# GNN and mixture-of-experts layer: VectorE takes all the scaling and adding ahead of the routing, with w2's loads and the counts moved

## The reference, cut to what matters

```python
x = x + gnn(layernorm(x), edges)            # x: 6250 x 256, 100000 edges, 8 heads of 32
x = x + ffn(layernorm(x)[None])[0]

def gnn(x, ...):                            # attention over the edges, summed by target node
    out = segment_sum(attn_exp * h[src], dst) / (segment_sum(attn_exp, dst) + 1e-10)
    return out + x
def ffn(x, ...):                            # 16 experts, hidden 512, top 2
    gate_logits = x @ gate_w + gate_b
    topk_vals, topk_idx = top_k(gate_logits, 2)
    moe = sum_k softmax(topk_vals)_k * (relu(x @ w1[e_k] + b1[e_k]) @ w2[e_k] + b2[e_k])
    return layernorm(x + moe) * gamma + beta
```

## Time and profile before

| | |
|---|---|
| median of 3 runs | 1956.9 us (1956.38 to 1959.61) |
| the profiled execution | 1957.13 us, of which its span 1955.3 us |
| sum over edges ends, routing stage begins | about 1326.5 us from the start of the span |
| first gather of rows by slot issued | 1456.3 us |
| `layer2` of the first slot tile begins | 1471.4 us |
| busy over the span | PE 78%, POOL 61%, DVE 60%, ACT 40% |

### The profile page before, as it was taken

The page is one execution under the profiler, slowest core; times in us unless marked ns, Lnnn a source line. Parts: engine busy times, 40 slices in busy tenths (PEclk is TensorE's granted clock), DMA queues, the critical chain, the costliest instruction groups (busy, mean ns, idle before and its releaser), DMA issues.

```text
span 1955.3 us, 28026 instructions
## 1 busy us (share of the span) xinstructions
PE 1515.8 (78%) x6735; PEld 1115.6 (57%) x6735; DVE 1177.6 (60%) x3451; ACT 774.8 (40%) x2346; POOL 1200.1 (61%) x1186
## 2 busy tenths in 40 slices
PE   7647777777777777777777777774959999999976
PEld 5524444444444444444444444443848999999963
DVE  7746666666666666666666666669873444333338
ACT  3434444444444444444444444342622333333326
POOL 1366666666666666666666666637354767656757
PEclk9856666666766666676666667675559999999987
DMA  8544444444444444444444444422957878888876
GB/s 240 151 113 119 114 113 116 115 120 116 113 115 115 121 117 112 115 117 118 120 111 116 116 118 118 112 60 89 281 162 191 220 212 212 211 205 206 220 170 199
DMA packets 167873, 283.93 MB, mean 145 GB/s; under 512 B 31671, under 2 KB 94504, under 8 KB 167592
## 3 DMA queue, kind: packets, MB, share of 16 engines
q0 software_dynamic: 62144, 143.99, 31.3%
q1 hardware_dynamic: 104532, 138.03, 23.0%
q10 hardware_dynamic: 1044, 0.13, 0.0%
HBM read 240.71 MB, written 42.16 MB: 145 GB/s over the span
## 4 chain that ended last, share of the span: by engine, by line
PE 64%; DVE 22%; issue 7%; DVEq 4%; another core or an unknown queue 2%; DMA 1%; ACT 0%; SPq 0%; ACTq 0%; POOL 0%; POOLq 0%
PE bank L1063 29%; PE bank L1204 10%; PE bank L1216 10%; DVE region L1533 5%; PE bank L1052 4%; PE bank L1088 2%; DVE region L1531 2%; DVE z L1486 2%; DVEq L496 2%; PE bank L993 2%; PE bank L1049 2%; PE bank L1113 2%; DVE z L1493 1%; DVE z L1498 1%
## 5 line engine op out<-in xcount | busy, mean ns | idle before, releaser
L898 POOL DMA_INDIRECT region<-node_rows,region x832 | 788.2, 947 | 449.1 <-issue 221.5
L1063 PE MATMUL bank<-region 128*128 128x264 f32 x1664 | 740.0, 593 | 70.9 <-DVE region L1533 68.0
L1063 PEld LDWEIGHTS bank<-region 128*128 128x128 f32 x1664 | 440.1, 290 | 211.6 <-issue 124.9
L1533 DVE TENSOR_TENSOR region<-region,bank 128x264 f32 x728 | 310.6, 427 | 343.3 <-PE bank L1063 261.1
L756 ACT ACTIVATE neg_max<-bank 128x1 f32<-128x1 f32 x104 | 17.8, 171 | 711.7 <-PE bank L1088 588.1
L1519 DVE TENSOR_TENSOR region<-region,bank 128x512 f32<-128x512 f32 x416 | 265.2, 678 | 7.9 <-issue 7.9
L746 ACT ACTIVATE region<-iota_row,region 128x128 f32<-128x128 f32 x832 | 262.7, 386 | 0.0
L830 ACT ACTIVATE region<-bank,b_col 128x128 f32<-128x128 f32 x452 | 128.7, 368 | 311.9 <-PE bank L1204 224.1
L974 POOL DMA_INDIRECT sum_rows<-region,row_u x113 | 179.6, 1590 | 111.8 <-DVE region L1953 52.8
L1204 PEld LDWEIGHTS bank<-region 128*128 128x128 f32 x1808 | 220.3, 192 | 6.3 <-issue 0.4
L1204 PE MATMUL bank<-region 128*128 128x128 f32 x1808 | 220.8, 275 | 0.2 <-issue 0.2
(11 more groups left out here) (247 smaller groups left out, 1619.4 us busy)
## 6 DMA issues: line engine op xcount, KB each, us to landing
region<-in_L_ffn_w SPq DMA_DIRECT2D x129, 512.0 KB, 8.3
region<-dloc_rows SPq DMA_DIRECT2D x104, 256.0 KB
region<-node_rows,region POOLq DMA_INDIRECT x832
node_rows<-region SPq DMA_DIRECT2D x12, 528.0 KB, 4.0
y_rows<-region SPq DMA_DIRECT2D x7, 896.0 KB, 6.0
sum_rows<-region SPq DMA_DIRECT2D x7, 896.0 KB, 7.5
region<-in_x SPq DMA_DIRECT2D x5, 896.0 KB, 11.0
region<-sum_rows SPq DMA_DIRECT2D x5, 896.0 KB, 11.2
```

What stands on the lines that cost most here:

```text
L898: p.indirect_dma_start(gathered[g % SLOTS][:, j, :], None, node_rows, bass.IndirectOffsetOnAxis(src_idx[:, k:k + 1], 0)).then_inc(row_in[g ...
L1063: pe.matmul(bank[AGG_BANKS[k % AGG]][:, 0:ROW], onehot[:, (g % 3) * GROUP + j, :], gathered[g % SLOTS][:, j, :], start=True, stop=True).th ...
L1533: v.tensor_tensor(rows, rows, new, ALU.add).then_inc(acc_add)
```

## The change

DVE scales and adds all eight groups, in their order, and POOL none of them. The second part of the inverted sums is now tiles 7 to 13, the third tiles 14 to 48. The normalised rows get a third buffer, in the place of the gathered rows of the first seven tiles, so ACT waits for the store of three batches before, not two. SP stores all seven batches of rows first; then it waits until all additions are made, loads experts 2 to 12 of w2, waits until the batches in the third buffer have left it, and loads experts 0 and 1. Experts 13 to 15 are loaded ahead of the stage as before. In DVE's program `best_two(0)` and `choose(0)` stand behind the variance of group 7 instead of group 6. In PE's program the count of set 0 stands in group 7 behind its fifth tile's transposes (before: in group 5), and that of set 1 behind the last tile of the gate (before: in group 7, fourth tile).

```diff
-C_DVE, C_POOL = (0, 1, 2, 4), (3, 5, 6, 7)
-C_PARTS = ((0, 7), (14, TILES), (7, 14))
+C_DVE = (0, 1, 2, 3, 4, 5, 6, 7)
+C_PARTS = ((0, 7), (7, 14), (14, TILES))
+Y_RING = 3
...
-        y_all = region2[:, 0:2 * BATCH * F_IN].rearrange("p (s t f) -> p s t f", s=2, f=F_IN)
+        Y_AT = (region2[:, 0:BATCH * F_IN], region2[:, BATCH * F_IN:2 * BATCH * F_IN], region1[:, 0:BATCH * F_IN])
+        y_all = [y.rearrange("p (t f) -> p t f", f=F_IN) for y in Y_AT]
...
-            w2_at = 0
             for q in range(BATCHES):
                 store_y0(q)
-                i = q + 1
-                if i in C_POOL:
-                    d.wait_ge(x1_pool, 2 * C_POOL.index(i) + 2)
-                else:
-                    d.wait_ge(x1_dve, 2 * C_DVE.index(i) + 2)
-                while w2_at < behind_sums and (q == BATCHES - 1 or (w2_at + 1) * FC * F_IN <= (q + 1) * BATCH * ROW):
-                    load_w2(w2_at)
-                    w2_at += 1
+            d.wait_ge(x1_dve, len(X1))
+            behind_y = -(-BATCH * F_IN // (FC * F_IN))
+            for expert in range(behind_y, behind_sums):
+                load_w2(expert)
+            for q in range(BATCHES):
+                if q % Y_RING == 2:
+                    d.wait_ge(y_out[2], y_landed(q))
+            for expert in range(behind_y):
+                load_w2(expert)
...
-                if q >= 2:
-                    s.wait_ge(y_out[q % 2], y_landed(q - 2))
+                if q >= Y_RING:
+                    s.wait_ge(y_out[q % Y_RING], y_landed(q - Y_RING))
...
-            for n in range(len(C_POOL)):
-                residual(n)
...
-                    if i == 5 and t == t0 + 3:
+                    if i == 7 and t == t0 + 4:
                         count_choices(0)
-                    if i == 7 and t == t0 + 3:
-                        count_choices(1)
                 gate_logits(t1 - 1)
+            count_choices(1)
...
-            sums_part(1)
+            gathered_sums(1)
             shift_c(0)
-            inverse_sums(1)
-            gathered_sums(1)
             add_x(1)
             stats_c(1)
-            sums_part(2)
-            inverse_sums(2)
+            sums_part(1)
+            inverse_sums(1)
             shift_c(1)
             gathered_sums(2)
             add_x(2)
             stats_c(2)
-            stats_c(3, 2)
+            sums_part(2)
+            shift_c(2)
+            inverse_sums(2)
+            gathered_sums(3)
+            add_x(3)
+            stats_c(3)
             gathered_sums(4)
             shift_c(3)
             add_x(4)
             stats_c(4)
+            gathered_sums(5)
+            shift_c(4)
+            add_x(5)
             stats_c(5)
-            shift_c(4)
+            gathered_sums(6)
+            shift_c(5)
+            add_x(6)
             stats_c(6)
+            gathered_sums(7)
+            shift_c(6)
+            add_x(7)
+            stats_c(7)
             best_two(0)
-            shift_c(5)
+            shift_c(7)
             choose(0)
-            stats_c(7)
-            shift_c(6)
             v.wait_ge(pool_consts, POOL_CONSTS["empty"])
             v.tensor_copy(empty, empty_i).then_inc(c_const_step)
             slots(0)
             for q in range(*SETS[0]):
                 tile_hots(q)
-            shift_c(7)
             pair_firsts(0)
```

More of the change, by code:

```diff
@@ L52 @@
 FC = HIDDEN // P
-assert sum(C_TILES) == TILES and sorted(C_DVE + C_POOL) == list(range(len(C_TILES)))
+assert sum(C_TILES) == TILES and sorted(C_DVE) == list(range(len(C_TILES)))
 assert TILES % BATCH == 0 and SLOT_TILES <= P and ROW <= 512
@@ L301, in build_program @@
         late_step, late_exp, late_mm = sem("late_step"), sem("late_exp"), sem("late_mm")
-        y_out = [sem(f"y_out{i}") for i in range(2)]
-        sums_step, x1_dve, x1_pool = sem("sums_step"), sem("x1_dve"), sem("x1_pool")
+        y_out = [sem(f"y_out{i}") for i in range(Y_RING)]
+        sums_step, x1_dve = sem("sums_step"), sem("x1_dve")
         y0_ok, y0_tr, y0t_ok = sem("y0_ok"), sem("y0_tr"), sem("y0t_ok")
@@ L339, in build_program @@
         SUMS = at([(name, n) for n in range(len(C_PARTS)) for name in ("sums", "rsum")])
+        X1 = at([("scaled", 0), ("added", 0), ("scaled", 1), ("added", 1), ("scaled", 2), ("added", 2),
+                 ("scaled", 3), ("added", 3), ("scaled", 4), ("added", 4), ("scaled", 5), ("added", 5),
+                 ("scaled", 6), ("added", 6), ("scaled", 7), ("added", 7)])
         WEIGHT = at([("gap", 0), ("gap", 1)] + [(n, s) for s in range(2) for n in ("gap1", "weight0", "weight1")])
@@ L402, in y_landed @@
         def y_landed(q):
-            return 32 * (q // 2 + 1) + (16 if q % 2 == 0 else 0)
+            return 32 * (q // Y_RING + 1) + (16 if q % Y_RING == 0 else 0)
         A_NORMS = len(A_TILES)
@@ L451, in p_bank @@
             return bank[Z_BANKS[g % 2]][:, GROUP * AD:GROUP * (AD + HEADS)].rearrange("p (j h) -> p j h", h=HEADS)
-        y_all = region2[:, 0:2 * BATCH * F_IN].rearrange("p (s t f) -> p s t f", s=2, f=F_IN)
+        Y_AT = (region2[:, 0:BATCH * F_IN], region2[:, BATCH * F_IN:2 * BATCH * F_IN], region1[:, 0:BATCH * F_IN])
+        assert BATCH * F_IN <= C_PARTS[0][1] * ROW
+        y_all = [y.rearrange("p (t f) -> p t f", f=F_IN) for y in Y_AT]
         yt_buf = region2[:, 2 * BATCH * F_IN:2 * BATCH * F_IN + 2 * F_IN].rearrange("p (s f) -> p s f", f=F_IN)
@@ L597, in store_y0 @@
                 d.wait_ge(y0_ok, (q + 1) * BATCH)
-                d.dma_start(rows_of(y0_rows, q)[:, :, 0:F_IN], y_all[:, q % 2, :, :]).then_inc(y_out[q % 2], 16)
-                d.dma_start(rows_of(sum_rows, q), y_all[:, q % 2, :, :]).then_inc(y_out[q % 2], 16)
+                y = y_all[q % Y_RING]
+                d.dma_start(rows_of(y0_rows, q)[:, :, 0:F_IN], y[:, :, :]).then_inc(y_out[q % Y_RING], 16)
+                d.dma_start(rows_of(sum_rows, q), y[:, :, :]).then_inc(y_out[q % Y_RING], 16)
             def store_weights(s):
@@ L644, in sync_program @@
             d.wait_ge(slot_step, SLOT["expert_row"])
-            for q in (BATCHES - 2, BATCHES - 1):
-                d.wait_ge(y_out[q % 2], y_landed(q))
+            for q in range(BATCHES - Y_RING, BATCHES):
+                d.wait_ge(y_out[q % Y_RING], y_landed(q))
             experts = None
@@ L781, in norm @@
                 q = t0 // BATCH
-                if q >= 2:
-                    s.wait_ge(y_out[q % 2], y_landed(q - 2))
+                if q >= Y_RING:
+                    s.wait_ge(y_out[q % Y_RING], y_landed(q - Y_RING))
                 for t in range(t0, t0 + n):
-                    s.activation(y_all[:, q % 2, t % BATCH, :], x_all[:, t, :], ACT.Identity,
+                    s.activation(y_all[q % Y_RING][:, t % BATCH, :], x_all[:, t, :], ACT.Identity,
                                  bias=shift[:, t:t + 1], scale=rstd[:, t:t + 1]).then_inc(y0_ok)
@@ L899, in gpsimd_program @@
                                          bass.IndirectOffsetOnAxis(src_idx[:, k:k + 1], 0)).then_inc(row_in[g % SLOTS], 16)
[L902 to L913, removed]
             def choice_one_hots(q):
@@ L949, in gpsimd_program @@
             p.wait_ge(slot_step, SLOT["token"])
-            for q in (BATCHES - 2, BATCHES - 1):
-                p.wait_ge(y_out[q % 2], y_landed(q))
+            for q in range(BATCHES - Y_RING, BATCHES):
+                p.wait_ge(y_out[q % Y_RING], y_landed(q))
             p.wait_ge(weight_out, 32)
@@ L1124, in norm_transposes @@
                     ins = pe.transpose(bank[4 + t % 2][:, c * P:(c + 1) * P],
-                                       y_all[:, t // BATCH % 2, t % BATCH, c * P:(c + 1) * P], ident[:, :])
+                                       y_all[t // BATCH % Y_RING][:, t % BATCH, c * P:(c + 1) * P], ident[:, :])
                 ins.then_inc(y0_tr)
@@ L1612, in gathered_sums @@
                 hv = acc_t[:, t0:t1, 0:F_IN].rearrange("p t (h o) -> p t h o", o=F_OUT)
-                v.wait_ge(sums_step, SUMS["rsum", 0 if t1 <= C_PARTS[0][1] else 2 if t1 <= C_PARTS[2][1] else 1])
+                v.wait_ge(sums_step, SUMS["rsum", [n for n, part in enumerate(C_PARTS) if part[0] <= t0 < part[1]][0]])
                 v.tensor_tensor(hv, hv, rsum[:, t0:t1, :].unsqueeze(3).broadcast_to([P, t1 - t0, HEADS, F_OUT]),
@@ L1620, in add_x @@
                     v.wait_ge(s_ok, TILES)
-                v.wait_ge(x1_dve, 2 * C_DVE.index(i) + 1)
+                v.wait_ge(x1_dve, X1["scaled", i])
                 v.tensor_tensor(x_all[:, t0:t1, :], acc_t[:, t0:t1, 0:F_IN], x_all[:, t0:t1, :],
@@ L1626, in stats_c @@
                 t0, n = c_first[i], C_TILES[i]
[L1627 to L1630, removed]
+                v.wait_ge(x1_dve, X1["added", i])
                 for t in range(t0, t0 + n + 1):
```

## The result

The changed kernel takes 1961.48 us (median of 15 runs, 1960.07 to 1964.59). The kernel before, run between them on the same chip, takes 1957.84 us (1956.38 to 1960.53). The ratio is 1.0022, with a 95% interval of 1.0015 to 1.0029: slower by 3.6 us. The forecast was 1961.0 us, 4.1 us over the 1956.9 us that the kernel before had then.

What follows compares the result with a forecast made beforehand. From 1418.9 to the first gather everything moves with DVE, so its second count decides: 1957.13 + 4.8 - 0.7 + 0 + 0 = 1961.2, against the median 1961.0 us; 8 in 10 range 1955.0 to 1964.5.

Steps and rivals of the forecast that it cites:

- The new bound of the gate: Gate: DVE has group 3's variance at 1353.5, then PE sets the pace, 8.74 us a group; gate 14 us ahead.
- The counts later: Routing stage: later counts start slots(0) at 1401.8, 6.9 us later, and slots(1) at 1419.6, 4.8 us later.
- The second wait and the 0.71 us: DVE's wait for set 1's count is 2.7 us; its 0.71 us wait before the tables goes, leaving 4.1 us.
- cover: Time POOL's one-hots, ending at 1443.0, have to spare before they delay DVE's tables of batch 5: 1.4 us.
- POOL becomes the bound: Rival, 13%: POOL's one-hot batches take 36.3 us instead of 33.8, use up the spare time and give 1962.1 to 1963.5 us.
- w2 and the third buffer: w2 loads behind the stores land by 1430 at 278 GB/s; that and the third buffer were both priced at nothing.
- The clock did not rise: Gate: PE's clock stays at 0.50; the rival, full clock, had 6% and would give about -4 us, 1952.9 us.
- The unknown stretch: 20.4 us before the expert loop on nothing known, expected unchanged; rival, 14%: some 4 us of it goes, 1956.9 us.
- the scaling at 1363.06: DVE's scaling in the kernel before, read as not slowed by POOL since it took 2.01 us beside it.
- The layout: The forecast's time plan of DVE, PE and ACT through the routing stage, POOL idle; error about 2.5 us each way.

Runs made afterwards that it cites:

- e_count0_early: c_after with PE's count of set 0 three tiles earlier in group 7; 1967.41 us, ratio 1.0048 to the kernel before.
- e_choices_early: c_after with set 0's choices behind group 5's variance and group 6's shift, its count in group 6; 1959.96 us, ratio 1.0005 to the kernel before.
- e_before_late: The kernel before, with enforced wait bounds, given the change's late places of choices and counts; 1981.83 us, ratio 1.012 to the kernel before.
- e_pool_more: c_after with 8 more one-hots on POOL ahead of its third batch, into an unused place; 1977.03 us, ratio 1.009 to the kernel before.
- c_after: The changed kernel with GpSimd enforcing bounds on its loaded wait values in the expert loop; 1970.27 us, ratio 1.0057 to the kernel before.

## Why the prediction was right, point by point

**The size: right, a little by luck.** The forecast was +4.1 us on 1956.9, and +3.6 on 1957.84 was measured. That 1961.0 lies within 0.5 us of 1961.48 owes something to the kernel before being 0.9 us slower in the later runs.

**The new bound of the gate: right.** DVE had group 3's variance at 1353.1 (forecast 1353.5), PE began group 3 at 1358.28 (1358.6) and group 7 at 1393.21 (1393.6), at 8.73 us a group (8.74). The one duration taken over from the earlier trace rows, 5.14 us from ACT's root to PE's next group, measured 5.15.

**The counts later: right, and it is the cause.** The scan of set 0 came at 1401.37 (1401.8) and that of set 1 at 1419.83 (1419.6). DVE's wait was 9.40 us, where the forecast had 8.4, since DVE was ready at 1391.97, not 1393.4. Of these 1.4 us the waits for ACT's roots account for 0.6 (1.9 us in all, not 2.5); I have not divided the rest. On the path nothing changes by that, since PE sets the time of the scan. That the second scan is only 0.2 us off is two misses that cancel: the first scan came 0.4 us early, and from there to the end of `choose(1)` DVE took 15.67 us, 15.15 forecast. `e_count0_early`, `e_choices_early` and `e_before_late` show the cause: three tiles of the place are worth 3.6 us, choices and count made early 10.0, the whole move without DVE's gain 16.6.

**The second wait and the 0.71 us: right.** 2.53 us against 2.7, and 0.71 us gone. From here the path gave 4.3 us at the last tables and at the gather, 4.1 forecast.

**POOL: right, with a little less cover.** It ended its one-hots at 1442.86 (1443.0). The cover is 1.1 us by `e_pool_more`, 1.4 forecast. The forecast took it from the end of the one-hots to DVE's tables, which measured 1.7; PE's products stand between and take 0.6 of it. The rival "POOL becomes the bound" was only a microsecond away.

**w2 and the third buffer: right at nothing.** The loads were over by 1430 as forecast, though at 348 GB/s for 278, and undoing either part moves the gather by 0.1 us.

**The clock did not rise: right.** It was 0.50 over the 19.21 of 19.30 us that PE was busy from 1360 to 1379.3, and all the way to the gather. The Trainium skill, page "TensorE: Matmul & The Clock Gate", section "What's actually happening", says that sustained activity releases the throttle, and by that rule it would have gone to 2.4 GHz; this trace again does not agree. In `e_choices_early` it did rise for a few us behind the count, with no effect on the gather.

**The unknown stretch: right that it stays.** 20.34 against 20.39 us. I had one candidate for its 4 us, and the runs rule it out.

**One reading was wrong, without effect.** The prediction took the scaling at 1363.06 for work that POOL does not disturb, since it took 2.01 us. POOL's rows in the kernel before show that there POOL was the one that stood:

```profile
1345.24 5.73 POOL L912 TENSOR_TENSOR region<-region 128x1792 f32<-128x1792 f32 x1
1350.92 5.00 POOL L909 TENSOR_TENSOR region<-region,rsum 128x1792 f32<-128x1792 f32 x1
1355.99 3.96 POOL L912 TENSOR_TENSOR region<-region 128x1792 f32<-128x1792 f32 x1
1359.91 3.21 POOL L909 TENSOR_TENSOR region<-region,rsum 128x1792 f32<-128x1792 f32 x1
1363.20 5.71 POOL L912 TENSOR_TENSOR region<-region 128x1792 f32<-128x1792 f32 x1
```

The additions of 5.73 and 5.71 us began 0.13 and 0.14 us behind a scaling of DVE (1345.11 and 1363.06, 2.01 us each); the one of 3.96 us did not. The other way round, DVE's addition at 1347.15 began behind POOL's at 1345.24 and took 5.70 us. In each of these pairs the one that began second paid. The layout is not touched, since POOL is idle in it.

## What to carry to other kernels

What is won by relieving an engine that sets the pace early in a stage is lost again if the same edit puts the hand-over, on which the stage's end depends, later in another engine's written order: move the hand-over up to where the relief makes its input ready, and only then measure. Where one edit holds two large terms of opposite sign (here +16.6 and -12.1 us), time at least one with the other undone, since a small total hides both. And a chain that names an engine is not yet a bound: adding a known amount of work to it tells how many microseconds it is away.

## What the runs showed of the hardware that was not expected

GpSimd's one-hots of 14 x 128 x 128 took 8.7, 11.2 and 11.0 us in the three batches, and 9.07 in `e_pool_more`. Most single ones take 0.60 us; in `c_after`'s third batch one took 2.42, and DVE wrote its own tables (L1733, 2.08 us) at that time. In `e_pool_more` the one of 2.42 us was again beside that work of DVE, and the batch without it was 2 us shorter. So the duration of a batch can't be carried over when the work moves.

Enforcing bounds on the loaded wait values in the expert loop cost 6 to 8 us in all, with DVE's wait for scattered rows up from 58.5 to 93.2 us in the kernel before and from 64.4 to 125.6 in the changed one, though GpSimd had time to spare in that loop (210.57 of 320 us busy from 1480 to 1800 in `c_after`).
